# Two graph sum passes: VectorE's one-hots wait for the rows of the unit two ahead in line

## The chip, the cores and the metric

The kernel runs on one core of one Trainium2 chip. The metric is the device time of one launch in microseconds, the median of the runs shown.

## What is computed

The reference is a four-layer graph network on 3,125 nodes of 256 features and 100,000 edges. Each layer adds a graph part, a mixing part and a feed-forward part to x. The change touches the graph parts of layers 1 and 2 alone, which are sums over edges:

```python
# layer 1
index = row * N_EDGE_TYPE + edge_type
sums = segment_sum(x[col], index, num_segments=n * N_EDGE_TYPE)
cnt  = segment_sum(ones, index, num_segments=n * N_EDGE_TYPE)
out1 = (sums / maximum(cnt, 1)[:, None]).reshape(n, -1) @ weights
# layer 2
msgs = (x @ W)[row] * norm[:, None]
out2 = segment_sum(msgs, col, num_segments=N) + bias
```

## The kernel before

The edges are sorted by the node that they are summed into (in layer 1 by `src`, in layer 2 by `dst`) and cut into units of 4 chunks of 128 edges. All edges of a unit belong to one tile of 125 nodes. There are 220 units (`UNITS_S`). In layer 1 the table rows are already multiplied by the weights of each edge type, and the mean's share is the weight of the edge. Both layers then run the same function, `build_sums` (L585): layer 1 with the table `rel_table`, layer 2 with the table `el`.

Inside `build_sums` three engines work on the units in order, each with a program written out by hand:

- GpSimd (L593 to L603) issues four indirect DMAs for a unit, one a chunk, that gather 128 rows of 256 floats each into the row buffer u % 10 (`LANES_S`). From the eleventh unit on it first waits for `batch_summed` of the unit ten before, so that the buffer is free. Each DMA raises the semaphore `rows_in` of its buffer by 16.
- VectorE (L605 to L634) makes a unit's four one-hots with `make_hot` (L611): a 128 x 125 matrix a chunk that holds the edge's weight in the column of its node. There are 14 buffers of them (`HOTS_S`). `add` (L619) takes the finished sum of the unit ten before (`BEHIND`) out of PSUM and adds it to the tile's rows in `acc`; at the first unit of a batch of four it waits for `batch_summed`. After each turn VectorE raises `step` by one. VectorE's loop makes the one-hots of unit n and then adds unit n - 10.
- TensorE (L636 to L643) waits for `step` and for the unit's `rows_in`, multiplies the four one-hots with the four row blocks into one PSUM slot of 16, and raises `batch_summed` after every fourth unit (`BATCH`).

So VectorE may make one-hots ahead of the rows, as far as its own additions let it: it stops at the first addition whose batch isn't summed.

Of the kernel before, what the change touches and what calls it, by code (L numbers as in the profile page):

```python
# [16 lines left out]
G = 4  # L17
# [15 lines left out]
LANES_S = 10  # L33
BATCH = 4
HOTS_S = 14
SLOTS_S = 16
BEHIND = 10
HOTS = 4
REC = 4
REC_LANES = 8  # L40
# [39 lines left out]
@contextmanager  # L80
def phase(nc, tag, *names):

    sems = {n: nc.alloc_semaphore(f"{tag}_{n}") for n in names}
    yield sems
    nc.clear_and_free_semaphores(list(sems.values()))
    nc.all_engine_barrier()


def row_of(ap, k):

    return ap.unsqueeze(1).to_broadcast([ap.shape[0], k, ap.shape[1]])


def col_of(ap, n):

    return ap.unsqueeze(2).to_broadcast([ap.shape[0], ap.shape[1], n])
# [483 lines left out]
def batches_of(u):  # L580

    return u // BATCH + 1


def build_sums(nc, c, tag, table, o, w, acc):  # L585

    assert UNITS_S % BATCH == 0 and HOTS_S >= BEHIND + BATCH and SLOTS_S >= BEHIND + BATCH and BATCH % 2 == 0
    with ExitStack() as ctx:
        rows = [ctx.enter_context(nc.sbuf_tensor(f"{tag}_rows{l}", [P, G, D], F32)) for l in range(LANES_S)]
        hot = [ctx.enter_context(nc.sbuf_tensor(f"{tag}_hot{l}", [P, G, R], F32)) for l in range(HOTS_S)]  # L590
        banks = [ctx.enter_context(nc.psum_tensor(f"{tag}_sum{l}", [R, 2, D], F32)) for l in range(SLOTS_S // 2)]
        slot = lambda u: banks[u % SLOTS_S // 2][:, u % 2, :]
        with phase(nc, tag, "cleared", "batch_summed", "step", *[f"rows_in{l}" for l in range(LANES_S)]) as s, nc.Block() as block:  # L593
            @block.gpsimd
            def _(pool):
                for u in range(UNITS_S):
                    l = u % LANES_S
                    if u >= LANES_S:
                        pool.wait_ge(s["batch_summed"], batches_of(u - LANES_S))
                    for g in range(G):  # L600
                        k = u * G + g
                        nc.gpsimd.indirect_dma_start(rows[l][:, g, :], None, table, bass.IndirectOffsetOnAxis(ap=o["row"][:, k:k + 1], axis=0)  # L602
                                                     ).then_inc(s[f"rows_in{l}"], 16)  # L603

            @block.vector  # L605
            def _(dve):
                v = nc.vector
                v.memset(acc[:], 0.0).then_inc(s["cleared"], 1)

                def make_hot(u):  # L610
                    if u >= HOTS_S:  # L611
                        dve.wait_ge(s["batch_summed"], batches_of(u - HOTS_S))
                    for g in range(G):
                        k = u * G + g
                        last = v.tensor_scalar(hot[u % HOTS_S][:, g, :], c["iota"][:, 0:R], o["node"][:, k:k + 1], w[:, k:k + 1], ALU.is_equal, ALU.mult)
                    return last

                def add(u, steps):
                    at = dve.value_load(o["tile"][0:1, u:u + 1], min_val=0, max_val=TILES - 1)  # L619
                    to = acc[:, bass.ds(at, 1), :].rearrange("p t d -> p (t d)")  # L620
                    if u % BATCH == 0:
                        dve.wait_ge(s["batch_summed"], batches_of(u))
                    dve.wait_ge(s["step"], steps)
                    return v.tensor_tensor(to, to, slot(u), ALU.add)  # L624

                dve.wait_ge(s["cleared"], 1)
                for n in range(UNITS_S + BEHIND):
                    if n < UNITS_S:
                        last = make_hot(n)
                    if n >= BEHIND:  # L630
                        last = add(n - BEHIND, n)
                    last.then_inc(s["step"], 1)

            @block.tensor  # L634
            def _(pe):
                for u in range(UNITS_S):  # L636
                    l = u % LANES_S
                    pe.wait_ge(s["step"], u + 1)
                    pe.wait_ge(s[f"rows_in{l}"], 16 * G * (u // LANES_S + 1))
                    for g in range(G):  # L640
                        last = nc.tensor.matmul(slot(u), hot[u % HOTS_S][:, g, :], rows[l][:, g, :], start=(g == 0), stop=(g == G - 1))  # L641
                    if u % BATCH == BATCH - 1:
                        last.then_inc(s["batch_summed"], 1)  # L643
# [22 lines left out]
def mark_hots(nc, c, o, u, hot):  # L666

    return nc.vector.tensor_tensor(hot[u % HOTS][:], row_of(c["iota"][:, 0:R], G), col_of(o["node"][:, u * G:u * G + G], R), ALU.is_equal)

# [6 lines left out]
def build_attend0(nc, c, o, table, to_dst, attn, acc, pairs):  # L676
# [9 lines left out]
    with ExitStack() as ctx:  # L686
        sb = lambda n, sh, d=F32: ctx.enter_context(nc.sbuf_tensor(f"att0_{n}", sh, d))
        ps = lambda n, sh: ctx.enter_context(nc.psum_tensor(f"att0_{n}", sh, F32))
        rows, hot = [sb(f"rows{l}", [P, G, S]) for l in range(LANES_A)], [sb(f"hot{l}", [P, G, R]) for l in range(HOTS)]
        hot_t, mask = [sb(f"hot_t{l}", [R, G * P]) for l in range(TURNED)], [sb(f"mask{l}", [R, G * P]) for l in range(TURNED)]  # L690
# [8 lines left out]
        with phase(nc, "att0", *names) as s, nc.Block() as block:  # L699
# [11 lines left out]
            def _(dve):  # L711
# [7 lines left out]
                def make_hot(u):  # L719
                    if u >= HOTS:  # L720
                        dve.wait_ge(s["summed"], u - HOTS + 1)
                    mark_hots(nc, c, o, u, hot).then_inc(s["hot_ready"], 1)
# [59 lines left out]
            def _(pe):  # L782
                t = nc.tensor

                def turn(u):
# [3 lines left out]
                    for g in range(G):  # L789
                        last = t.transpose(turn_p[:, g * P:(g + 1) * P], hot[u % HOTS][:, g, :], c["ident"][:])  # L790
                    last.then_inc(s["turned"], 1)
# [27 lines left out]
                def add_up(u):  # L819
# [3 lines left out]
                    for g in range(G):  # L823
                        last = t.matmul(sums[u % 2][:, 0:S], hot[u % HOTS][:, g, :], rows[u % LANES_A][:, g, :], start=(g == 0), stop=(g == G - 1))  # L824
                    last.then_inc(s["summed"], 1)
# [2526 lines left out]
```

## Time and profile before

| what | us |
|---|---|
| median of 3 runs | 9699.5 |
| lowest, highest | 9695.85, 9704.59 |
| span of the profiled execution | 10401.4 |
| layer 1: first gather to last addition | 3754.8 to 5012.9 |
| layer 2: first gather | 5544.5 |
| GpSimd busy with gathers of one sum pass | 833.0 |
| TensorE busy with matmuls of both sum passes | 1227.5 |

The profiled execution is one run on its own; its span is longer than the timed runs. Its own time beside the span isn't among the numbers shown. In the timeline a line is a run of equal instructions: its start, its length, the engine, the line in the program, the operation, what it writes and reads, their count, and in brackets how long the engine was idle before it and what ended that.

### The profile page before, as it was taken

How to read it: one execution, taken by the hardware profiler on the slowest of the kernel's cores; microseconds unless marked ns; L12 is line 12 of the kernel's file. 1: busy time of each engine (PE TensorE's matmuls, PEld its weight loads, DVE VectorE, ACT ScalarE, POOL GpSimd, SP SyncE). 2: the span in 40 equal slices, each digit the busy share in tenths (PEclk: the TensorE clock that was granted, in tenths of full speed). 3: DMA queues.
4: the chain of work that ended last, by engine and by line, in shares of the span. 5: the costliest groups of instructions: out<-in, count | busy, mean ns of one | idle time of the engine just before them, and what ended most of it. 6: DMA issues, size and time to landing. Idle time of an engine off the chain costs nothing. (4 is left out here: it accounts for less than half of the span.)

```text
span 10401.4 us, 95746 instructions
## 1 busy us (share of the span) xinstructions
PE 6311.5 (61%) x28050; PEld 4795.7 (46%) x28050; DVE 4856.6 (47%) x13537; ACT 2031.2 (20%) x5038; POOL 4458.2 (43%) x4412
## 2 busy tenths in 40 slices
PE   0001115999996865454665444453965788887699
PEld 0000004888884433333443333342863676776466
DVE  7561216888884532222242222264113566666633
ACT  0000002444443210000120000012212232232322
POOL 0546772666660036666104666602020566664000
PEclk9998557999997986666676666675987777777799
DMA  0001002333330133333102333301960232222000
GB/s 12 6 1 28 7 4 71 83 83 83 83 83 14 46 108 92 94 92 92 35 11 70 94 92 92 92 18 25 316 221 27 77 81 80 80 81 64 11 13 19
DMA packets 404431, 697.45 MB, mean 67 GB/s; under 512 B 154143, under 2 KB 267784, under 8 KB 403421
## 3 DMA queue, kind: packets, MB, share of 16 engines
q0 software_dynamic: 206848, 480.68, 17.1%
q1 hardware_dynamic: 197076, 210.68, 6.3%
q8 instruction: 236, 3.87, 0.2%
q14 instruction: 271, 2.22, 0.1%
HBM read 631.46 MB, written 59.47 MB: 66 GB/s over the span
## 5 line engine op out<-in xcount | busy, mean ns | idle before, releaser
L658 POOL DMA_INDIRECT att_rows<-el_table,dst_order_row x1520 | 1589.4, 1046 | 1067.4 <-issue 387.0
L641 PE MATMUL sum_sum<-sum_rows,sum_hot 128*125 128x256 f32 x3520 | 1227.5, 487 | 1291.4 <-issue 817.1
L641 PEld LDWEIGHTS sum_sum<-sum_rows,sum_hot 128*125 128x125 f32 x3520 | 824.8, 240 | 1694.4 <-issue 1540.9
L602 POOL DMA_INDIRECT sum_rows<-rel_table,src_order_row x880 | 833.0, 947 | 1042.3 <-ACTq L593 629.2
L602 POOL DMA_INDIRECT sum_rows<-el_table,dst_order_row x880 | 833.0, 947 | 956.7 <-ACTq L593 543.7
L554 POOL DMA_INDIRECT dst_order_record<-records,dst_order_row x784 | 813.7, 1038 | 589.2 <-PEq L458 297.1
L624 DVE TENSOR_TENSOR gnn_acc<-gnn_acc,sum_sum 125x256 f32 x440 | 180.6, 410 | 1888.8 <-DMA ffn1e_w<-in_L_ffn_W_dram 938.7
L1136 PE MATMUL att_sum<-att_rows,att_hot 128*125 128x265 f32 x1280 | 429.3, 492 | 36.4 <-ACT att_part L1203 30.5
L800 PE MATMUL att_found<-gnn_to_dst,att_hot_t 125*128 x1760 | 437.8, 392 | 2.5 <-ACT att_hot_t L849 1.8
L658 POOL DMA_INDIRECT dst_order_record<-el_table,dst_order_row x240 | 266.1, 1109 | 400.4 <-SPq L960 240.5
L824 PE MATMUL att_sum<-att_rows,att_hot 128*125 128x261 f32 x1760 | 427.3, 385 | 2.4 <-ACT att_rows L862 2.4
L862 ACT ACTIVATE att_rows<-att_rows,att_p 128x257 f32<-128x257 f32 x880 | 375.8, 498 | 0.0
L1101 PEld LDWEIGHTS att_found<-layer_a_dst,att_hot_t 125*128 125x128 f32 x1760 | 275.9, 227 | 180.6 <-issue 159.4
L1136 PEld LDWEIGHTS att_sum<-att_rows,att_hot 128*125 128x125 f32 x1280 | 293.4, 241 | 114.7 <-issue 46.9
L1101 PE MATMUL att_found<-layer_a_dst,att_hot_t 125*128 x1760 | 254.4, 268 | 140.1 <-issue 84.2
L800 PEld LDWEIGHTS att_found<-gnn_to_dst,att_hot_t 125*128 125x128 f32 x1760 | 319.7, 192 | 38.0 <-issue 3.1
L824 PEld LDWEIGHTS att_sum<-att_rows,att_hot 128*125 128x125 f32 x1760 | 314.2, 188 | 47.8 <-ACT att_rows L862 2.5
L744 DVE CUSTOM_DVE_ANT_0 att_high<-att_high,att_att 128x256 f32<-128x256 f32 x880 | 320.0, 418 | 0.0
L1162 ACT COPY att_hot_t<-att_turn_p 125x512 f32<-125x512 f32 x220 | 129.1, 587 | 802.7 <-PE att_turn_p L1091 461.7
L809 PE MATMUL att_spread_p<-ident,att_score 128*125 128x128 f32 x1760 | 251.6, 286 | 43.2 <-issue 27.2
L739 DVE TENSOR_TENSOR att_high<-att_rows,att_found 128x1024 f32<-128x1024 f32 x220 | 268.7, 1222 | 6.5 <-issue 6.5
L809 PEld LDWEIGHTS att_spread_p<-ident,att_score 128*125 128x125 f32 x1760 | 210.0, 188 | 130.6 <-issue 85.1
(775 smaller groups left out, 12593.2 us busy)
## 6 DMA issues: line engine op xcount, KB each, us to landing
block_w<-in_L_ffn_W_dram SPq DMA_DIRECT2D x112, 512.0 KB, 6.3
block_w<-in_L_ffn_W_dram SPq DMA_DIRECT2D x56, 1024.0 KB
att_rows<-el_table,dst_order_row POOLq DMA_INDIRECT x1520
rel_table<-open_st SPq DMA_DIRECT2D x25, 784.0 KB
sum_rows<-rel_table,src_order_row POOLq DMA_INDIRECT x880
sum_rows<-el_table,dst_order_row POOLq DMA_INDIRECT x880
dst_order_record<-records,dst_order_row POOLq DMA_INDIRECT x784
pairs<-zeros SPq DMA_DIRECT2D x1, 7168.0 KB
```

The source lines that it names most:

```text
L554: nc.gpsimd.indirect_dma_start(o["record"][:, k, :], None, o["records"], bass.IndirectOffsetOnAxis(ap=o["row"][:, k:k + 1], axis=0)).then_ ...
L602: nc.gpsimd.indirect_dma_start(rows[l][:, g, :], None, table, bass.IndirectOffsetOnAxis(ap=o["row"][:, k:k + 1], axis=0)).then_inc(s[f"row ...
L641: last = nc.tensor.matmul(slot(u), hot[u % HOTS_S][:, g, :], rows[l][:, g, :], start=(g == 0), stop=(g == G - 1))
L658: nc.gpsimd.indirect_dma_start(rows[l][:, g, 0:width], None, table, bass.IndirectOffsetOnAxis(ap=o["row"][:, k:k + 1], axis=0)).then_inc(s ...
L739: v.tensor_tensor(high[:], rows[u % LANES_A][:, :, 0:D], found[:], ALU.max).then_inc(s["picked"], 1)
L744: last = v.tensor_tensor_reduce(high[:, g, :], high[:, g, :], att[:], 0.8, 0.0, ALU.mult, ALU.add, score[u % 2][:, g:g + 1])
L800: last = t.matmul(found[:, g, :], hot_t[u % TURNED][:, g * P:(g + 1) * P], nodes_of_unit(to_dst, tile), start=True, stop=True)
L809: last = t.matmul(spread_p[:, g * P:(g + 1) * P], score[u % 2][:, g:g + 1].to_broadcast([P, R]), c["ident"][:], start=True, stop=True)
L824: last = t.matmul(sums[u % 2][:, 0:S], hot[u % HOTS][:, g, :], rows[u % LANES_A][:, g, :], start=(g == 0), stop=(g == G - 1))
L862: last = a.activation(own_rows[:, g, 0:D + 1], own_rows[:, g, 0:D + 1], ACT.Copy, scale=p[u % 2][:, g:g + 1])
L1101: done = t.matmul(found[u % 2][:, g, 0:H], hot_t[u % 2][:, g * P:(g + 1) * P], nodes_of_unit(to_dst, tile), start=True, stop=True)
L1136: done = t.matmul(sums[u % SUMS_B][:, 0:W + 1], hot[u % HOTS_B][:, g, :], rows[u % LANES_B][:, g, :], start=(g == 0), stop=(g == G - 1))
```

## The change

A constant `AHEAD_S = 2` is added. In `make_hot(u)` VectorE waits, from the third unit on, until all four gathers of unit u - 2 have landed, which is 64 increments of that unit's `rows_in` for each use of its buffer. It stands behind the existing wait for a free one-hot buffer and ahead of the four one-hots.

```diff
+AHEAD_S = 2
...
                 def make_hot(u):
                     if u >= HOTS_S:
                         dve.wait_ge(s["batch_summed"], batches_of(u - HOTS_S))
+                    if u >= AHEAD_S:
+                        at = u - AHEAD_S
+                        dve.wait_ge(s[f"rows_in{at % LANES_S}"], 16 * G * (at // LANES_S + 1))
                     for g in range(G):
```

All engines keep their instructions in the same order. What changes on VectorE are the places where it waits. These are VectorE's instructions at the beginning of layer 1's pass, before the change; the name of a semaphore is that of the first stage that used its number, so that `records_stored` stands for `batch_summed` and `dst_sort_chain` for `step`, and x43 is a run of 43 one-hots:

```order
L608 MEMSET gnn_acc 125x6400
L615 TENSOR_SCALAR sum_hot<-iota,src_order_node,src_order_w 128x125 [waits constants_chain]
L615 TENSOR_SCALAR sum_hot<-iota,src_order_node,src_order_w 128x125 x43
L619 TENSOR_LOAD src_order_tile
L619 ISA x2
L624 ISA [waits dst_sort_chain,records_stored]
L624 TENSOR_TENSOR gnn_acc<-gnn_acc,sum_sum 125x256
```

The one-hots of eleven units stand in one run, up to the first addition. The same place after the change, where `open0_kept`, `open0_flipped` and `open0_xt_ready` are `rows_in` of the first three buffers:

```order
L609 MEMSET gnn_acc 125x6400
L619 TENSOR_SCALAR sum_hot<-iota,src_order_node,src_order_w 128x125 [waits constants_chain]
L619 TENSOR_SCALAR sum_hot<-iota,src_order_node,src_order_w 128x125 x7
L619 TENSOR_SCALAR sum_hot<-iota,src_order_node,src_order_w 128x125 [waits open0_kept]
L619 TENSOR_SCALAR sum_hot<-iota,src_order_node,src_order_w 128x125 x3
L619 TENSOR_SCALAR sum_hot<-iota,src_order_node,src_order_w 128x125 [waits open0_flipped]
L619 TENSOR_SCALAR sum_hot<-iota,src_order_node,src_order_w 128x125 x3
L619 TENSOR_SCALAR sum_hot<-iota,src_order_node,src_order_w 128x125 [waits open0_xt_ready]
L619 TENSOR_SCALAR sum_hot<-iota,src_order_node,src_order_w 128x125 x3
```

The run is cut into one of eight one-hots, for units 0 and 1, and then runs of four, each behind a wait for the rows of the unit two before.

## Rows read from the trace of the kernel before

**Rows 1.** The page's head.

```profile
span 10401.4 us, 95746 instructions
```

**Rows 2.** Groups by line, 3754 to 5015: out<-in xcount | busy, mean ns | idle before.

```profile
L602 POOL DMA_INDIRECT sum_rows<-rel_table,src_order_row x880 | 833.0, 947 | 1042.3 <-ACTq L593 629.2 <-issue 259.8 <-DMA ffn0e_w<-in_L_ffn_eW_dram 153.3
L615 DVE TENSOR_SCALAR sum_hot<-iota,src_order_node,src_order_w 128x125 f32<-128x125 f32 x880 | 253.4, 366 | 0.0
L624 DVE TENSOR_TENSOR gnn_acc<-gnn_acc,sum_sum 125x256 f32 x220 | 90.2, 410 | 944.4 <-DMA ffn0e_w<-in_L_ffn_eW_dram 907.6 <-issue 31.9 <-PE sum_sum L641 2.4
```

**Rows 3.** Waits of GpSimd, 3754 to 5015: us in total, times, longest.

```profile
POOL sum_rows L602 <- issue: 259.8, 853, 0.3
POOL sum_rows L602 <- DMA ffn0e_w<-in_L_ffn_eW_dram: 153.3, 26, 8.9
```

**Rows 4.** Line 602 in both passes: durations in ns min/median/max; one of its waits.

```profile
L602 POOL DMA_INDIRECT sum_rows<-rel_table,src_order_row x880: 940/946/1027, 3754.8 to 4999.8; - x176
L602 POOL DMA_INDIRECT sum_rows<-el_table,dst_order_row x880: 940/946/1042, 5544.5 to 6789.5; - x176
...
  DMA ffn1e_w<-in_L_ffn_W_dram: 153.2, 26
```

**Rows 5.** Timeline of all engines, the beginning of layer 1's pass.

```profile
3754.79 0.95 POOL L602 DMA_INDIRECT sum_rows<-rel_table,src_order_row  x1 [629.22 <-ACTq L593]
...
3760.98 11.33 DVE L615 TENSOR_SCALAR sum_hot<-iota,src_order_node,src_order_w 128x125 f32<-128x125 f32 x44
...
3762.14 3.78 PE L641 MATMUL sum_sum<-sum_rows,sum_hot 128*125 128x256 f32 x8 [12.41 <-DVE sum_hot L615]
3762.30 0.99 POOL L602 DMA_INDIRECT sum_rows<-rel_table,src_order_row  x1 [0.30 <-issue]
3763.59 0.95 POOL L602 DMA_INDIRECT sum_rows<-rel_table,src_order_row  x1 [0.30 <-issue]
...
3766.46 3.75 PE L641 MATMUL sum_sum<-sum_rows,sum_hot 128*125 128x256 f32 x8 [0.55 <-DMA sum_rows<-rel_table,src_order_row]
...
3773.73 0.94 POOL L602 DMA_INDIRECT sum_rows<-rel_table,src_order_row  x1 [0.30 <-issue]
```

**Rows 6.** The same timeline, TensorE a little later.

```profile
3781.54 1.96 PE L641 MATMUL sum_sum<-sum_rows,sum_hot 128*125 128x256 f32 x8 [1.59 <-DMA sum_rows<-rel_table,src_order_row]
...
3786.75 3.24 PE L641 MATMUL sum_sum<-sum_rows,sum_hot 128*125 128x256 f32 x8 [3.25 <-DMA sum_rows<-rel_table,src_order_row]
```

**Rows 7.** Stretches: length, busy us (records) by engine, granted clock, DMA share, GB/s.

```profile
core 0: us, PE busy (x) PEld busy (x) DVE busy (x) ACT busy (x) POOL busy (x), PEclk, DMA share, GB/s
3762.10:3770.20 8.10, 7.51 (x16) 4.95 (x16) 8.10 (x33) 0.00 (x0) 6.08 (x7) 0.50 0.34 97
...
3797.60:3833.00 35.40, 9.49 (x17) 4.25 (x15) 5.83 (x20) 0.00 (x0) 20.64 (x22) 0.50 0.29 85
3856.00:3877.00 21.00, 4.86 (x9) 2.56 (x9) 0.00 (x0) 0.00 (x0) 13.22 (x14) 0.50 0.32 94
```

**Rows 8.** Timelines of VectorE and GpSimd around 3879.

```profile
3878.92 0.42 DVE L624 TENSOR_TENSOR gnn_acc<-gnn_acc,sum_sum 125x256 f32 x1 [33.96 <-DMA ffn0e_w<-in_L_ffn_eW_dram]
...
3880.28 0.41 DVE L624 TENSOR_TENSOR gnn_acc<-gnn_acc,sum_sum 125x256 f32 x1
...
3888.85 1.22 DVE L615 TENSOR_SCALAR sum_hot<-iota,src_order_node,src_order_w 128x125 f32<-128x125 f32 x4
...
3879.05 0.95 POOL L602 DMA_INDIRECT sum_rows<-rel_table,src_order_row  x1 [5.79 <-DMA ffn0e_w<-in_L_ffn_eW_dram]
```

**Rows 9.** Timeline of all engines, the end of layer 1's pass.

```profile
4992.83 2.47 PE L641 MATMUL sum_sum<-sum_rows,sum_hot 128*125 128x256 f32 x5 [2.39 <-DMA sum_rows<-rel_table,src_order_row]
...
4999.84 0.95 POOL L602 DMA_INDIRECT sum_rows<-rel_table,src_order_row  x1 [0.30 <-issue]
...
5011.73 0.42 DVE L624 TENSOR_TENSOR gnn_acc<-gnn_acc,sum_sum 125x256 f32 x1 [0.34 <-DVE gnn_acc L624]
5012.49 0.42 DVE L624 TENSOR_TENSOR gnn_acc<-gnn_acc,sum_sum 125x256 f32 x1 [0.34 <-DVE gnn_acc L624]
```

## The prediction

> **What bounds the kernel now.** I read the page first: the profiled execution spans 10401.4 us [rows 1]. The timed runs have a median of 9699.5 us, 701.9 us less, so the profile tells mechanisms and the sum below is a difference, made on the profiled execution and carried to the median. Then the groups by line over the first sum pass. It starts with the first gather at 3754.79 us and ends with the last addition at 5012.9 us [rows 5, 9]. GpSimd issues 880 gathers (L602) of 947 ns and stands idle 259.8 us "issue" between them, 0.30 us each [rows 2, 3]. A unit of four gathers so takes 4 x (0.947 + 0.30) = 4.99 us, and 220 units take 1,098 us. The other 153 us are 26 waits of GpSimd, which the waits view puts down to an unlikely DMA of another stage; what GpSimd waits for there in the code is `batch_summed` [rows 3]. The second pass has the same two figures, 947 ns and 153.2 us [rows 4]. Next the timeline: TensorE begins a unit when its rows have landed, 5.0 us after the one before, and is done with its 8 records in 1.96 us at the full clock, or 3.78 us at half [rows 5, 6]. VectorE is busy 253.4 + 90.2 us of the pass, 1.56 us a unit, and idle for 944 us [rows 2]. So the chain is GpSimd's issue, and behind it TensorE by way of `batch_summed` 26 times in a pass. VectorE is on neither.
>
> One thing in the trace needs care. TensorE has stretches in which it hardly moves: in 21.0 us from 3856 it does 9 matmul records at a granted clock of 0.50 (the 1.2 GHz level), while 16 records at the same clock fit in 8.1 us earlier [rows 7]. So the low level alone doesn't explain them. GpSimd runs out of freed row buffers in each and waits, most often 5.8 us, as at 3879.05 [rows 8]; that is where the 26 waits come from. VectorE shows no busy time at all from 3856 to 3877 [rows 7].
>
> **The change, part by part.** First, 218 waits are added to each pass, one ahead of a unit's four one-hots (units 0 and 1 have none). No instruction changes its place. Behind the wait on VectorE stand the four one-hots of unit n, then the addition of unit n-10, and then the `step` increment for which TensorE waits. The trace of before has no such wait. A wait at which VectorE really sleeps can be bounded by the tail, where additions follow one another 0.76 us apart with 0.34 us idle between two, a self-wait and a register load [rows 9]. A step of VectorE in a burst takes 1.35 us (3878.92 to 3880.28) [rows 8]; with the wait it is 1.35 to 1.69 us (1.35 + 0.34), and a unit has 4.99 us. Its own cost is hidden by GpSimd's issue: 0 us. Without that cover it would be up to 218 x 0.34 = 74 us a pass.
>
> Second, the lead of the one-hots falls. Now VectorE makes 11 units of them in one go (44 in 11.33 us) [rows 5], and later steps on in bursts of eight from 3878.92 to 3890.07, as often as batches come free [rows 8]. After the change the one-hots of unit u begin when the rows of u-2 land and are announced at most 1.69 us later. The rows of u land 2 x 4.99 = 9.98 us after those of u-2. That leaves 9.98 - 1.69 = 8.3 us of slack in every unit: TensorE still waits for the rows last. When TensorE lags, rows are landed far ahead, so the new wait is met already and the older wait, the one for `batch_summed` in the addition, holds VectorE as now. I put 0 us, and 0 to both sides of it: a step of 1.69 us ends before the next rows in any case.
>
> Third, the additions. The addition of unit n-10 stands behind the one-hots of unit n, so it now waits for the rows of n-2 too. Its only reader within the pass is the reuse of a sum slot 16 units on, which is six units later than that addition; and the tail. At the tail, the last gather ends at 5000.79 [rows 9] and its rows land about 1.9 us behind it (unit 1's last issue ended at 3764.54, TensorE began it at 3766.46 [rows 5]), so at 5002.7; those of unit 217 at 5002.7 - 9.98 = 4992.7, and TensorE does begin a unit at 4992.83 [rows 9]. From there VectorE has its last one-hots, 1.69 us, and six additions of 0.76 us, 4.6 us, before those of the last batch: done at 4999.0, 3.7 us before the last rows land. So again 0; if all six were left over, 2 x 4.6 = 9 us for both passes.
>
> Fourth, VectorE beside GpSimd. Issues in the opening burst of one-hots read up to 0.99 us, against 0.94 us once it is over [rows 5], so an issue beside one-hots can cost up to 0.05 us. A burst of four steps is 5.4 us long and touches about 6 issues of 1.25 us; four single steps touch about 2 each, 8. That is 2 more in four units, 110 in a pass, 5.5 us, and 11 us for both passes at most. Below nothing: if spreading took all disturbance away, 947 would become the shortest issue, 940 ns [rows 4], -7 ns x 880 x 2 = -12 us. I take 0: the mean of now, 947, stands 1 ns from the median, 946 [rows 4], so issues beside one-hots weigh little already.
>
> The Trainium skill speaks against the change here: "SBUF — State Buffer", section "Who interferes with whom", says that VectorE's tensor_scalar can enter a two-port mode that locks GpSimd out of a shared port pair for the whole instruction, descriptors of its DMAs included. By that rule each of the 110 newly touched issues could wait a whole one-hot, 0.366 us, 40 us a pass and 81 us for both. The opening burst, 44 one-hots back to back under nine issues, shows 0.05 us and not 0.37, so the trace doesn't bear out a lock of that size.
>
> The sum: 0 + 0 + 0 + (-12 to +11), so 0 on the profiled execution, and 9,700 us for the timed median.
>
> **Rivals.** (a) *VectorE disturbs GpSimd* (slower). If one-hots spread over the whole pass held every one of the 880 issues at 0.99 us in place of 0.947, a pass would be 38 us longer and the kernel 76 us: 9,776 us. It leaves the bound of no change, 19.4 us or 9.7 us a pass, once a further quarter of the issues (9.7 / 38) is held; my count above gives a further eighth (110 of 880). For it: GpSimd's issue is the bound, so each nanosecond counts. Against: VectorE is busy 1.4 of 4.99 us and can't touch all four issues of a unit. The skill's lock ends at much the same time, 9,781 us, and is in this case's chance. (b) *The bursts cause TensorE's slow stretches* (faster). They come 26 times in 220 units, once in eight or nine, and the bursts are of eight steps; one-hots paced by landings would end the bursts. If the stretches are there in the timed runs too, their 153.3 + 153.2 = 306.5 us would go: 9,393 us. Against: the first stretch, at 3797.6 [rows 7], came 25 us after the opening burst had ended (3760.98 + 11.33) [rows 5]; VectorE is idle in the one from 3856 [rows 7]; and the timed runs are 702 us shorter than the profiled one, so that these stalls may be no part of them. A half effect, at 9,550, is in this case. (c) *The wait never ends last for anybody* (no change): if VectorE were late anyway, the wait would be met when reached. The 44 one-hots in a row speak against it for the opening; the time would be the same 9,700 us, so it shares the forecast's side. (d) Something that I don't see lengthens the slow stretches, which already free buffers too late: one gather more in each of the 52 waits, 1.25 us, is 65 us, 9,765 us.
>
> **How the numbers follow.** Forecast, with (c) in it: 0.80. (a) 0.06, (b) 0.10, (d) 0.04. The bound between change and no change is 0.2%, 19.4 us, about what the measurement tells from nothing. My own terms reach from -12 to +11 us, and the runs of before spread from 9695.85 to 9704.59, so the forecast's range is 9,700 - 20 to 9,700 + 20, within the bound on both sides; the rivals, 0.20 together, are left out of it. Hence faster 0.10, same 0.80, slower 0.10.
>
> **What would show it.** Right: in the timeline VectorE's opening shows 8 one-hots and then fours at a distance of 5 us; the additions stand one by one between them; L602 stays at 947 ns give or take 10, and the groups show no idle time of TensorE put down to one-hots beyond the opening of each pass (12 us now). Each step wrong: L602's mean over 0.96 us (fourth part); TensorE idle for `sum_hot` in mid-pass (second); a last addition more than 5 us later behind the last matmul than now (third). The forecast as a whole falls if the timed median leaves 9,680 to 9,720, above all if GpSimd's 26 waits in a pass become fewer or shorter and the timed runs follow, which would be (b).

## The result, and the profile after

The changed kernel takes 9714.98 us, the median of 20 runs (9709.41 to 9727.47). The kernel before takes 9697.58 us, also the median of 20 (9691.43 to 9708.34). The ratio is 1.0018, with a 95% interval of 1.0011 to 1.0024: 17.4 us more, inside the range of 9,680 to 9,720 us and inside the 0.2% that the prediction calls no change, but near its edge, and the interval reaches a little beyond it. The sum had been 0. There is an effect, small and surely above nothing, and it has to be found.

The execution that the rows ahead of the prediction come from, with its span of 10401.4 us [rows 1], was an unusual one: a second profiled execution of the kernel before, 9695.68 us with a span of 9693.6, is like the timed runs. I call it the second profile of before, and the comparisons below are made with it.

The page of the changed kernel, head:

```profile
span 9708.2 us, 96158 instructions
```

This profiled execution took 9709.96 us. The groups by line in the stretch of layer 1's sum pass, changed kernel (out<-in xcount | busy us, mean ns of one | idle before and what ended it), which answer to [rows 2]:

```profile
L603 POOL DMA_INDIRECT sum_rows<-rel_table,src_order_row x880 | 842.9, 958 | 896.1 <-ACTq L594 628.3 <-issue 265.6 <-PE sum_sum L645 2.1
...
L619 DVE TENSOR_SCALAR sum_hot<-iota,src_order_node,src_order_w 128x125 f32<-128x125 f32 x880 | 244.1, 359 | 782.8 <-DMA sum_rows<-rel_table,src_order_row 782.7
L628 DVE TENSOR_TENSOR gnn_acc<-gnn_acc,sum_sum 125x256 f32 x220 | 90.9, 413 | 10.4 <-PE sum_sum L645 6.3 <-DVE gnn_acc L628 3.0 <-issue 0.4
```

VectorE now waits for rows, 782.7 us of a pass. And the gather, which was issued in 947 ns, takes 958. The same line in the second pass, from the page:

```profile
L603 POOL DMA_INDIRECT sum_rows<-el_table,dst_order_row x880 | 844.5, 960 | 806.6 <-ACTq L594 538.8
```

The waits in the first pass, changed kernel (us in total, times, longest), which answer to [rows 3]:

```profile
DVE sum_hot L619 <- DMA sum_rows<-rel_table,src_order_row: 782.7, 217, 5.0
...
PE sum_sum L645 <- DMA sum_rows<-rel_table,src_order_row: 477.0, 218, 4.5
POOL sum_rows L603 <- issue: 265.6, 872, 0.3
...
PE sum_sum L645 <- DVE sum_hot L619: 12.4, 1, 12.4
...
POOL sum_rows L603 <- PE sum_sum L645: 2.1, 7, 0.3
```

TensorE waits for one-hots once, 12.4 us at the opening of the pass, as before [rows 5]; in mid-pass only rows hold it. GpSimd waits for nothing but its own issue. The 26 long waits of [rows 3] are not there. They are not there in the second profile of before either, as its groups by line show:

```profile
L602 POOL DMA_INDIRECT sum_rows<-rel_table,src_order_row x880 | 836.0, 950 | 899.6 <-ACTq L593 631.9 <-issue 265.0 <-PE sum_sum L641 2.7
L602 POOL DMA_INDIRECT sum_rows<-el_table,dst_order_row x880 | 835.5, 949 | 807.1 <-ACTq L593 539.3 <-issue 265.6 <-PE sum_sum L641 2.1
```

Of the 153 us in each pass nothing is left. So the change has not removed them: they belonged to that one execution. From the first gather to the last addition a pass takes 1110.4 and 1110.0 us in the second profile of before (in the first one 1258), and 1117.4 and 1120.7 us in the changed kernel: 7.0 + 10.7 = 17.7 us, as much as the 17.4 us measured; these two executions themselves differ by 14.6 us in span, so nothing is left for the rest of the kernel. The gathers' busy time has grown by 842.9 - 836.0 = 6.9 and 844.5 - 835.5 = 9.0 us, 15.9 of the 17.7. The rest lies behind the last gather of the second pass, which ends 8.5 us ahead of the last addition, and 6.7 us ahead of it before. So nearly all of the cost is in GpSimd's issue, the bound of the passes.

Where in the issue? The timeline of the changed kernel in mid-pass (start, length, engine, line, operation, count, idle before):

```profile
3611.26 0.95 POOL L603 DMA_INDIRECT sum_rows<-rel_table,src_order_row  x1 [0.30 <-issue]
3611.62 1.11 DVE L619 TENSOR_SCALAR sum_hot<-iota,src_order_node,src_order_w 128x125 f32<-128x125 f32 x4 [3.31 <-DMA sum_rows<-rel_table,src_order_row]
...
3611.66 1.96 PE L645 MATMUL sum_sum<-sum_rows,sum_hot 128*125 128x256 f32 x8 [1.52 <-DMA sum_rows<-rel_table,src_order_row]
3612.51 1.03 POOL L603 DMA_INDIRECT sum_rows<-rel_table,src_order_row  x1 [0.30 <-issue]
3612.65 0.41 DVE L628 TENSOR_TENSOR gnn_acc<-gnn_acc,sum_sum 125x256 f32 x1
3613.85 0.95 POOL L603 DMA_INDIRECT sum_rows<-rel_table,src_order_row  x1 [0.30 <-issue]
3615.10 0.95 POOL L603 DMA_INDIRECT sum_rows<-rel_table,src_order_row  x1 [0.30 <-issue]
3616.35 0.95 POOL L603 DMA_INDIRECT sum_rows<-rel_table,src_order_row  x1 [0.30 <-issue]
3616.67 1.11 DVE L619 TENSOR_SCALAR sum_hot<-iota,src_order_node,src_order_w 128x125 f32<-128x125 f32 x4 [3.62 <-DMA sum_rows<-rel_table,src_order_row]
...
3617.60 0.99 POOL L603 DMA_INDIRECT sum_rows<-rel_table,src_order_row  x1 [0.30 <-issue]
```

Of four issues one is longer, 1.03 and 0.99 us in place of 0.95, and in both units it is the one that starts while the last of the four one-hots runs. The four start 0.257 us apart, so the last one starts 0.77 us behind the first: at 3612.39 in the first unit, 0.12 us ahead of the issue at 3612.51, and at 3617.44 in the second, 0.16 us ahead of that at 3617.60. I took all 1760 issues of the two passes from the same records, and sorted those that start beside a unit's last one-hot by how far behind its start they begin:

| start behind the last one-hot's start, ns | issues | mean length, ns | longer than 960 ns |
|---|---|---|---|
| 80 to 100 | 27 | 1057 | 26 |
| 100 to 120 | 44 | 1043 | 44 |
| 120 to 140 | 78 | 1025 | 78 |
| 140 to 160 | 88 | 1005 | 88 |
| 160 to 180 | 93 | 985 | 93 |
| 180 to 200 | 53 | 967 | 42 |
| 200 to 220 | 19 | 949 | 0 |
| 220 to 260 | 14 | 946 | 0 |

An issue of 946 ns that starts in this window ends as if it had started 0.21 us behind the one-hot. With the middle of each range and the mean's excess over 946, 90 + 111, 130 + 79, 170 + 39, 190 + 21 are all near 210 ns. I call that lengthening the hold. Of the 1760 issues 372 are over 960 ns; in the second profile of before 118 are.

Why should nearly every unit meet it? VectorE's row of one-hots now begins at a landing (at 3611.62 the rows have landed, and TensorE begins the same unit at 3611.66); a landing follows the end of a unit's fourth issue by a steady time, and the issues follow one another in steps of 1.25 us. So the row stands at the same place between two issues in unit after unit. If that place is a bad one, it is bad some 200 times in a pass. Before, VectorE's rows come in bursts when a batch comes free, with four steps 1.35 us apart, and meet the issues at places that differ. This was the theory to test; the rivals were that the shorter lead of the one-hots costs the time, that the addition holds the issue, and that VectorE's work as such does, wherever it stands.

### The profile page after: what moved, and what is told of

Read it like the earlier page. It is cut to its first block and busy times, and to the rows that moved or that the text cites. A ratio compares the mean times of both kernels' runs of the same rounds, so it can differ in the third digit from the quotient of the medians.

```text
span 9708.2 us, 96158 instructions
## 1 busy us (share of the span) xinstructions
PE 6252.1 (64%) x28050; PEld 4787.4 (49%) x28050; DVE 4875.1 (50%) x13537; ACT 2039.2 (21%) x5038; POOL 4520.6 (47%) x4412
## 5 line engine op out<-in xcount | busy, mean ns | idle before, releaser
L645 PE MATMUL sum_sum<-sum_rows,sum_hot 128*125 128x256 f32 x3520 | 1256.6, 520 | 984.4 <-DMA sum_rows<-el_table,dst_order_row 484.0
L645 PEld LDWEIGHTS sum_sum<-sum_rows,sum_hot 128*125 128x125 f32 x3520 | 862.1, 257 | 1378.9 <-issue 1183.5
L603 POOL DMA_INDIRECT sum_rows<-rel_table,src_order_row x880 | 842.9, 958 | 896.1 <-ACTq L594 628.3
L603 POOL DMA_INDIRECT sum_rows<-el_table,dst_order_row x880 | 844.5, 960 | 806.6 <-ACTq L594 538.8
L555 POOL DMA_INDIRECT dst_order_record<-records,dst_order_row x784 | 834.8, 1065 | 582.5 <-PEq L459 297.0
L619 DVE TENSOR_SCALAR sum_hot<-iota,dst_order_node,dst_order_record 128x125 f32<-128x125 f32 x880 | 243.8, 357 | 783.9 <-DMA sum_rows<-el_table,dst_order_row 781.6
L619 DVE TENSOR_SCALAR sum_hot<-iota,src_order_node,src_order_w 128x125 f32<-128x125 f32 x880 | 244.1, 359 | 782.8 <-DMA sum_rows<-rel_table,src_order_row 782.7
L794 PE MATMUL att_turn_p<-ident,att_hot 128*125 128x128 f32 x880 | 155.1, 299 | 380.7 <-DVE att_hot L672 370.0
L794 PEld LDWEIGHTS att_turn_p<-ident,att_hot 128*125 128x125 f32 x880 | 113.5, 188 | 422.5 <-DVE att_hot L672 422.3
```

What stands on the lines that cost most here:

```text
L555: nc.gpsimd.indirect_dma_start(o["record"][:, k, :], None, o["records"], bass.IndirectOffsetOnAxis(ap=o["row"][:, k:k + 1], axis=0)).then_ ...
```

## The experiments

**The kernel before, once more.** No edit.

> The kernel before, unchanged, to have its profile from the same chip. Phase theory: GpSimd's gathers in the sum passes (L602) have a mean of about 947 ns against 958 and 960 ns in the changed kernel, 11 to 13 ns x 880 or 10 to 12 us a pass, which is the whole measured difference of 17.4 us within some 5 us. If the first profile's slow stretches of TensorE were part of that one execution only, they are absent here, GpSimd has no waits of 5.8 us, and the span is near 9698 us; if they belong to the kernel, they are here again and the span is near 10400 us.

Measured: 9695.68 us, a span of 9693.6, no long waits of GpSimd. The gathers read 950 and 949 ns and not 947, so that 8 and 10 ns each are left for the change. The stretch from 3548 to 4640 us of this profile (length, busy us and records of PE, PEld, DVE, ACT, POOL, then granted clock, DMA share, GB/s):

```profile
3548.00:4640.00 1092.00, 626.09 (x1744) 429.88 (x1744) 308.46 (x1097) 0.00 (x0) 826.71 (x871) 0.76 0.36 105
```

TensorE does 1744 records in 1,092 us at a mean granted clock of 0.76, where [rows 7] had 9 in 21 us at 0.50. The slow stretches of the first profile are not in this execution, whose time is that of the timed runs. VectorE still works in bursts; its timeline, second profile of before:

```profile
3608.15 0.42 DVE L624 TENSOR_TENSOR gnn_acc<-gnn_acc,sum_sum 125x256 f32 x1 [15.82 <-PE sum_sum L641]
3608.48 1.14 DVE L615 TENSOR_SCALAR sum_hot<-iota,src_order_node,src_order_w 128x125 f32<-128x125 f32 x4
3609.54 0.41 DVE L624 TENSOR_TENSOR gnn_acc<-gnn_acc,sum_sum 125x256 f32 x1
...
3626.50 0.42 DVE L624 TENSOR_TENSOR gnn_acc<-gnn_acc,sum_sum 125x256 f32 x1 [12.73 <-PE sum_sum L641]
```

One burst of four steps for each batch; ahead of these two VectorE was idle for 15.8 and 12.7 us, until TensorE had summed the next batch.

**The lead of the one-hots.** They wait for the unit six ahead instead of two, so that they are made four units earlier.

```diff
-AHEAD_S = 2
+AHEAD_S = 6
```

> AHEAD_S is 6 in place of 2: one-hots are made four units, some 20 us, earlier, but still when a unit's rows land. Phase theory (the last one-hot of a step stands over the start of a gather issue, because every step starts at the same distance behind a landing, and holds that issue by some 53 ns once a unit): no change against the kernel with 2, mean gather 956 to 961 ns, ratio to the kernel before 1.001 to 1.0025. Lead theory (two units are too little, TensorE gets its one-hots late): the loss goes, ratio 0.9995 to 1.0005.

Measured: 1.0017 [1.0008, 1.0026] against the kernel before, as slow as the change. The gather, from its groups by line:

```profile
L603 POOL DMA_INDIRECT sum_rows<-el_table,dst_order_row x880 | 843.5, 959 | 808.1 <-ACTq L594 540.4 <-issue 265.3 <-PE sum_sum L645 2.4
```

959 ns. A lead of six units helps nothing, so the lead was not what cost the time. Any landing has the same place among the issues, and the hold stays: 348 issues over 960 ns.

**The place of the row, moved.** A load of a tile number into a register that nobody reads, between the new wait and the one-hots, makes VectorE begin later and changes nothing else. I ran two loads first and then, with the reading below, one and three.

```diff
                         dve.wait_ge(s[f"rows_in{at % LANES_S}"], 16 * G * (at // LANES_S + 1))
+                        for _ in range(2):
+                            dve.value_load(o["tile"][0:1, u:u + 1], min_val=0, max_val=TILES - 1)
```

> The changed kernel, with two extra register loads on VectorE between the new wait and the one-hots, which move each step of VectorE about 1.1 us later within the same unit; the number of one-hots and of steps, and the pacing by landings, stay. Phase theory: the gather issue then begins some 250 to 400 ns behind the start of the last one-hot, not 80 to 200, and isn't held; mean gather 945 to 949 ns, ratio to the kernel before 0.9995 to 1.0006. Spread theory (every issue beside one-hots costs, and pacing spreads them over more issues): as the changed kernel or worse, 1.0015 or more. Lead theory: later one-hots are worse, 1.0018 or more.

Measured: 1.0017 [1.0008, 1.0026]. The hold did not go, and the expectation missed. The timeline of this kernel shows why:

```profile
3603.88 3.51 PE L647 MATMUL sum_sum<-sum_rows,sum_hot 128*125 128x256 f32 x8 [2.99 <-DMA sum_rows<-rel_table,src_order_row]
3604.79 0.95 POOL L603 DMA_INDIRECT sum_rows<-rel_table,src_order_row  x1 [0.30 <-issue]
3605.08 1.11 DVE L621 TENSOR_SCALAR sum_hot<-iota,src_order_node,src_order_w 128x125 f32<-128x125 f32 x4 [3.59 <-issue]
3606.04 0.97 POOL L603 DMA_INDIRECT sum_rows<-rel_table,src_order_row  x1 [0.30 <-issue]
```

The rows land by 3603.88, where TensorE begins, and the one-hots start at 3605.08: the two loads take 1.20 us. That is nearly the distance of two issues, 3606.04 - 3604.79 = 1.25 us. The row has moved by one whole step and meets the next issue at the same place: the last one-hot starts at 3605.85, 0.19 us ahead of the issue at 3606.04. If the theory holds, the effect is periodic: one load must remove the hold, and three must too.

The same edit with one load, `range(1)`:

> The changed kernel with one extra register load between the new wait and the one-hots, so that each step of VectorE comes about 0.6 us later, half the distance of 1.25 us between gather issues; two loads had moved it by nearly a whole distance, onto the start of the next issue. Phase theory: no issue starts while the last one-hot runs; mean gather 945 to 949 ns, sum passes of about 1104 us from first gather to the end of the last, 6 to 8 us less each than in the changed kernel, ratio to the kernel before 0.9988 to 1.0003. Spread theory: as the changed kernel, mean gather 957 to 961 ns and ratio 1.0015 or more.

Measured: 1.0001 [0.9992, 1.0010], and so no slower than before. The gathers of the first pass, and the timeline of this kernel in mid-pass:

```profile
L603 POOL DMA_INDIRECT sum_rows<-rel_table,src_order_row x880 | 832.1, 946 | 896.0 <-ACTq L594 628.2 <-issue 265.6 <-PE sum_sum L647 2.1
```

```profile
3604.54 3.54 PE L647 MATMUL sum_sum<-sum_rows,sum_hot 128*125 128x256 f32 x8 [3.02 <-DMA sum_rows<-rel_table,src_order_row]
3605.13 1.11 DVE L621 TENSOR_SCALAR sum_hot<-iota,src_order_node,src_order_w 128x125 f32<-128x125 f32 x4 [3.60 <-DMA sum_rows<-rel_table,src_order_row]
3605.43 0.94 POOL L603 DMA_INDIRECT sum_rows<-rel_table,src_order_row  x1 [0.30 <-issue]
3606.16 0.41 DVE L630 TENSOR_TENSOR gnn_acc<-gnn_acc,sum_sum 125x256 f32 x1
3606.68 0.94 POOL L603 DMA_INDIRECT sum_rows<-rel_table,src_order_row  x1 [0.30 <-issue]
```

The one-hots start 0.59 us behind the landing. The last one starts at 3605.90; the issues begin 0.47 us ahead of that and 0.78 behind, and both take 0.94. VectorE does the same instructions, and 218 loads a pass on top, and costs GpSimd nothing: that VectorE's work disturbs the issue wherever it stands is refuted. 13 issues of 1760 are over 960 ns. From the first gather to the end of the last one the passes take 1099.8 and 1100.2 us, 11 and 12 us less than in the changed kernel. That is more than the 6 to 8 us expected, since the smaller hold of the kernel before (1103.7 and 1103.3 us) is gone too.

The changed kernel again, one load and three loads, all beside the same runs of the kernel before:

> The changed kernel again, beside one and three register loads on the same chip. Phase theory: mean gather 956 to 962 ns, ratio to the kernel before 1.0010 to 1.0026, and slower than the kernels with one and three loads by 10 to 25 us. If the difference from the kernel with one load had come from the chip, it is gone here.

> One register load ahead of the one-hots, again, on the same chip as the changed kernel. Phase theory: mean gather 945 to 950 ns, ratio 0.9990 to 1.0005.

> Three register loads ahead of the one-hots, about 1.8 us. Phase theory: the effect is periodic in the distance of issues, 1.25 us: no load is held, one isn't, two are held, so three aren't; mean gather 945 to 950 ns, ratio 0.9990 to 1.0007. A theory in which a later step is simply better or worse has three as good as or worse than two loads by its own trend: two had 954 to 956 ns, better than none, so a smooth trend gives 950 to 953 ns for three, and 956 for one, where 946 was measured.

Measured: 1.0018 [1.0009, 1.0027] with no load, 1.0002 [0.9993, 1.0011] with one, 0.9994 [0.9985, 1.0003] with three. The gathers of the first pass with no load:

```profile
L603 POOL DMA_INDIRECT sum_rows<-rel_table,src_order_row x880 | 841.1, 956 | 892.4 <-ACTq L594 624.7 <-issue 265.3 <-PE sum_sum L645 2.4
```

The same group with three loads:

```profile
L603 POOL DMA_INDIRECT sum_rows<-rel_table,src_order_row x880 | 833.4, 947 | 892.3 <-ACTq L594 624.5 <-issue 265.0 <-PE sum_sum L647 2.7
```

On the same chip the changed kernel is 13 us slower than the one with one load and 21 us slower than the one with three, so the difference is not the chip's. With no load the issues are held, with one they are not, with two they are, with three they are not. Nor is it the number of issues that run beside a one-hot: in the trace with three loads 727 of 1760 overlap one and 40 are over 960 ns, in the second profile of before 539 and 118. It isn't how late the row is that decides, but its place within a step of 1.25 us.

**The kind of instruction.** The one-hots are made by an instruction that reads a second tile in SBUF (the weight as an operand of the whole row) in place of two scalars for each partition.

```diff
-                        last = v.tensor_scalar(hot[u % HOTS_S][:, g, :], c["iota"][:, 0:R], o["node"][:, k:k + 1], w[:, k:k + 1], ALU.is_equal, ALU.mult)
+                        last = v.scalar_tensor_tensor(hot[u % HOTS_S][:, g, :], c["iota"][:, 0:R], o["node"][:, k:k + 1], w[:, k:k + 1].to_broadcast([P, R]), ALU.is_equal, ALU.mult)
```

> The changed kernel with each one-hot made by a scalar_tensor_tensor whose weight comes as a broadcast tensor, so an instruction with two inputs from SBUF, in place of tensor_scalar with one; result and number are the same. If tensor_scalar's use of a port that GpSimd shares is what holds the issue (the Trainium skill, SBUF - State Buffer, Who interferes with whom, has tensor_scalar among the instructions that can take it), the hold goes or changes its size: mean gather 945 to 949 ns, ratio to the kernel before 0.9995 to 1.0006. If any VectorE instruction at that place holds the issue, or the second input takes the port as well, the mean gather stays at 955 to 962 ns and the ratio at 1.0012 to 1.0025.

Measured: 1.0022 [1.0013, 1.0031]. The timeline of this kernel:

```profile
3606.80 1.13 DVE L619 SCALAR_TENSOR_TENSOR sum_hot<-iota,src_order_node,src_order_w 128x125 f32<-128x125 f32 x4 [3.25 <-DMA sum_rows<-rel_table,src_order_row]
...
3607.75 1.00 POOL L603 DMA_INDIRECT sum_rows<-rel_table,src_order_row  x1 [0.30 <-issue]
```

The hold is as it was, 383 issues over 960 ns. So it is not particular to `tensor_scalar`. The Trainium skill, "SBUF — State Buffer", section "Who interferes with whom", names both forms: a `tensor_scalar` can enter a two-port mode, in which it takes the port pair that VectorE shares with GpSimd for its whole length if it is the first to issue, and an instruction with two inputs in SBUF contends with a GpSimd instruction that reads SBUF. Both runs agree with that in so far as GpSimd's issue is held (372 and 383 of 1760); neither shows that the port is the cause. A form that by that page takes no share of the pair was not tried, so the cause of the hold inside the two engines stays open.

**The addition.** VectorE adds first and makes the one-hots behind that, both behind the new wait. `wait_rows` is the wait of the change as a function; the part of the edit that is left out keeps it in `make_hot` for units 2 to 9, which have no addition.

```diff
...
                 for n in range(UNITS_S + BEHIND):
-                    if n < UNITS_S:
-                        last = make_hot(n)
                     if n >= BEHIND:
+                        if AHEAD_S <= n < UNITS_S:
+                            wait_rows(n)
                         last = add(n - BEHIND, n)
+                    if n < UNITS_S:
+                        last = make_hot(n)
```

> The changed kernel with each step of VectorE turned round: behind the wait for the rows comes the addition of the unit ten before, then the four one-hots, which so come some 0.33 us later. Phase theory: the issue starts while the third one-hot of four runs, with a fourth behind it; the last one-hot is over before the next issue starts; mean gather 945 to 952 ns and ratio 0.9990 to 1.0008. If it is the addition next to the issue's start that holds it and not the last one-hot, the hold goes too; then the few steps without an addition (units 2 to 9 of each pass) of the changed kernel should show no hold, and one of them does. Spread theory: as the changed kernel, 1.0015 or more.

Measured: 0.9993 [0.9984, 1.0002]. The timeline of this kernel:

```profile
3604.48 0.42 DVE L631 TENSOR_TENSOR gnn_acc<-gnn_acc,sum_sum 125x256 f32 x1 [3.63 <-DMA sum_rows<-rel_table,src_order_row]
3604.75 0.95 POOL L603 DMA_INDIRECT sum_rows<-rel_table,src_order_row  x1 [0.30 <-issue]
3604.82 1.10 DVE L622 TENSOR_SCALAR sum_hot<-iota,src_order_node,src_order_w 128x125 f32<-128x125 f32 x4
3606.00 0.95 POOL L603 DMA_INDIRECT sum_rows<-rel_table,src_order_row  x1 [0.30 <-issue]
```

An issue that starts 0.27 us behind the addition's start is not held, nor is the next one, which starts 0.41 us behind the last one-hot's. The mean of 949 ns is here the median too, and 11 issues are over 960. That the addition is not what holds the issue is seen also in the changed kernel itself, where unit 9 has no addition yet and the issue behind its last one-hot, begun 179 ns after that one's start, takes 973 ns. In its second pass the same holds for units 7 and 8, with 1017 and 982 ns.

**The wait once in a batch.** Only every fourth unit waits for rows; the other three follow as additions let them.

```diff
-                    if u >= AHEAD_S:
+                    if u >= AHEAD_S and u % BATCH == 0:
```

> The changed kernel with the new wait at every fourth unit alone, so that VectorE makes four units of one-hots in a burst whose start stands at a landing. Phase theory: of the sixteen issues of four units one or two start under the last one-hot of a step, against four in the changed kernel, since steps of 1.35 us drift against issues of 1.25 us; mean gather 947 to 953 ns, ratio to the kernel before 0.9995 to 1.0010. Spread theory: fewer issues beside one-hots than with single steps, the same direction, mean gather near the 949.9 ns of the kernel before.

Measured: 0.9998 [0.9989, 1.0007], gathers of 951 ns and 95 issues over 960 ns in both passes. With a quarter of the waits the bursts are back, and with them the number of before.

All profiled executions together. The passes are measured from the first gather to the last addition; "held" are issues over 960 ns of the 1760 of both passes, and "excess" the sum of all 1760 over their median (946 ns; 949 in the two that are marked):

| kernel | ratio to before | gather, mean ns, both passes | passes, us | held | excess, us |
|---|---|---|---|---|---|
| before, second profile | 1 | 950, 949 | 1110.4, 1110.0 | 118 | 6.5 |
| the change | 1.0018 [1.0011, 1.0024] | 958, 960 | 1117.4, 1120.7 | 372 | 22.4 |
| the change, again | 1.0018 [1.0009, 1.0027] | 956, 959 | 1117.1, 1120.0 | 352 | 20.1 |
| lead of six | 1.0017 [1.0008, 1.0026] | 957, 959 | 1117.9, 1119.6 | 348 | 20.4 |
| one load later | 1.0001 [0.9992, 1.0010] | 946, 946 | 1108.3, 1108.0 | 13 | -0.4 |
| one load later, again | 1.0002 [0.9993, 1.0011] | 946, 946 | 1106.7, 1108.0 | 11 | -0.3 |
| two loads later | 1.0017 [1.0008, 1.0026] | 954, 955 | 1114.7, 1116.7 | 306 | 15.7 |
| three loads later | 0.9994 [0.9985, 1.0003] | 947, 947 | 1108.4, 1109.0 | 40 | 1.5 |
| two inputs in SBUF | 1.0022 [1.0013, 1.0031] | 960, 962 | 1120.6, 1122.8 | 383 | 26.0 |
| addition first | 0.9993 [0.9984, 1.0002] | 949, 949 (949) | 1111.0, 1109.7 | 11 | -0.5 |
| wait once in a batch | 0.9998 [0.9989, 1.0007] | 951, 951 (949) | 1113.3, 1113.2 | 95 | 3.5 |

The kernels fall into two groups: those with 300 issues held and more are slower by 0.17 to 0.22%, with intervals that leave out 1; those with fewer than 120 have intervals that hold it. The change's excess over before's is 22.4 - 6.5 = 15.9 us, of 17.4 measured. Three loads and the addition first are the fastest, by 6 to 7 us in the middle of their intervals, which is about before's own excess of 6.5; but both intervals reach beyond 1, so no version here is shown to beat the kernel before.

**Which of the two waits.** The starts of VectorE's instructions in the same traces show another side of the hold. Of the issues that start 80 to 200 ns behind the start of any one-hot, 371 of 385 are over 960 ns in the changed kernel, but only 112 of 275 in the second profile of before. Beside 154 of the other 163 VectorE waits instead: its next instruction begins 0.18 us behind the start of the issue, and later than its usual step of 0.255 us. Both cases stand next to each other in the kernel that waits once in a batch:

```profile
3660.12 1.11 DVE L619 TENSOR_SCALAR sum_hot<-iota,src_order_node,src_order_w 128x125 f32<-128x125 f32 x4 [14.47 <-DMA sum_rows<-rel_table,src_order_row]
...
3661.07 0.97 POOL L603 DMA_INDIRECT sum_rows<-rel_table,src_order_row  x1 [0.30 <-issue]
...
3661.47 1.14 DVE L619 TENSOR_SCALAR sum_hot<-iota,src_order_node,src_order_w 128x125 f32<-128x125 f32 x4
3662.35 0.94 POOL L603 DMA_INDIRECT sum_rows<-rel_table,src_order_row  x1 [0.30 <-issue]
3662.53 0.41 DVE L628 TENSOR_TENSOR gnn_acc<-gnn_acc,sum_sum 125x256 f32 x1
```

The last one-hot of the first row starts at 3660.89, and the issue 0.18 us behind it takes 0.97. The last one of the second row starts at 3662.24; the issue 0.11 us behind it takes 0.94, the row is 1.14 us long in place of 1.11, and the addition begins 0.18 us behind the issue. In the first row of a burst, ahead of which VectorE was idle for over half a microsecond, 80 of 84 such issues are held in this kernel and 53 of 64 in the second profile of before; in later rows it is 9 of 210 and 59 of 211. In the changed kernel every row is a first row. So the bursts cost less in part because VectorE waits in most of their later rows, which costs nothing, as VectorE isn't the bound. What decides which of the two waits is not shown, and being a first row is not enough: with one load every row is one, and only 12 of 67 such issues are held.

## Why the prediction was right, and where its working was not

The forecast of no change held, and the time lies in the range. But the sum's own terms ended at +11 us, and 17.4 were measured. What held is the range, which was set at the bound of no change, 20 us to each side. To that extent it was luck.

*First, the cost of the wait itself.* Put at 0, and right. VectorE sleeps 217 times in the first pass, 782.7 us, and TensorE never waits for one-hots in mid-pass. The cover, GpSimd's issue of 5 us a unit, was there.

*Second, the lead.* Right: one wait for one-hots, 12.4 us, at the opening. The run with a lead of six, as slow as the change, shows that the lead isn't what cost the 17 us.

*Third, the additions and the tail.* Right. The end of the first pass in the changed kernel, which answers to [rows 9]:

```profile
4652.56 1.96 PE L645 MATMUL sum_sum<-sum_rows,sum_hot 128*125 128x256 f32 x8 [1.41 <-DMA sum_rows<-rel_table,src_order_row]
4654.67 0.42 DVE L628 TENSOR_TENSOR gnn_acc<-gnn_acc,sum_sum 125x256 f32 x1 [6.31 <-PE sum_sum L645]
...
4656.95 0.42 DVE L628 TENSOR_TENSOR gnn_acc<-gnn_acc,sum_sum 125x256 f32 x1 [0.34 <-DVE gnn_acc L628]
```

Four additions are left behind the last matmul, 0.76 us apart, and none of the six older ones.

*Fourth, VectorE beside GpSimd.* This is the term that was mis-sized. It said that an issue beside one-hots costs up to 0.05 us, that 110 more in a pass would be touched, and took 0 in a range of -12 to +11 us; it measured 15.9 us. Two things failed in it. The count took the touched issues as spread evenly and asked how many there are more. What decides is where beside a one-hot an issue starts, and which of the two then waits. The window is some 0.1 us wide of the 0.257 between two one-hots, and work paced by landings meets the issues at one place, in the window in most units or in few. In it start 385 issues of the changed kernel and 275 of the second profile of before; the larger difference is that 371 of the first and 112 of the second are held. Four single steps were counted to touch 8 issues for 6 of a burst; whether these 8 cost all or nothing could not be had from a count. And the price, 0.05 us, came from the opening burst [rows 5], whose issues begin at another place, the one of 0.99 us 36 ns behind a one-hot's start; in the window it goes up to 1057 - 946 = 0.11 us. The upper bound, had it taken one held issue in each of 218 units, would have been 218 x 0.11 x 2 = 48 us.

The sentence on the mean and the median of [rows 4], 947 and 946, from which I took that issues beside one-hots weigh little, rested on the unusual execution: there VectorE stood idle for long stretches [rows 7], and 212 issues began in the window, of which 58 were held, for 275 and 112 in the second profile. That one has 950 and 949 with the same median, 946.

The rule of the Trainium skill that spoke against the change ("SBUF — State Buffer", section "Who interferes with whom") had the direction right, which the prediction set aside. Its size, by the working of the prediction 81 us, is not what the runs show: a held issue waits not a whole one-hot of 0.36 us but until about 0.21 us behind its start, which is 0.11 us at most, and 17.7 us in all.

*The rivals.* (a) VectorE disturbs GpSimd: its mechanism is what happened, at less than a quarter of its price of 76 us; instead of every issue at 0.99 us, some 370 of 1760 are held, by 0.06 us on average (22.4 us / 372). The bound from which it was to decide, 9.7 us a pass or 19.4 for both, was just not reached: 7.0 + 10.7 = 17.7 us. (b) and (d), the slow stretches of TensorE: refuted by the second profile of before, which has the bursts, but neither stretches nor long waits. The prediction had seen that the timed runs were 702 us shorter than the profiled one and gave (b) 0.10 for that; it was right not to carry the 306 us to the timed runs. (c) The wait ends last nowhere: refuted, it ends VectorE's idle time 217 times in a pass.

*The signs that were named.* VectorE's opening shows twelve one-hots in one go and not eight, since VectorE clears `acc` until 3546.07 and the rows of unit 0 have landed before the first eight are done. Then come the fours, 5 us apart:

```profile
3546.11 3.15 DVE L619 TENSOR_SCALAR sum_hot<-iota,src_order_node,src_order_w 128x125 f32<-128x125 f32 x12
3551.40 1.11 DVE L619 TENSOR_SCALAR sum_hot<-iota,src_order_node,src_order_w 128x125 f32<-128x125 f32 x4 [2.14 <-DMA sum_rows<-rel_table,src_order_row]
3556.41 1.11 DVE L619 TENSOR_SCALAR sum_hot<-iota,src_order_node,src_order_w 128x125 f32<-128x125 f32 x4 [3.90 <-DMA sum_rows<-rel_table,src_order_row]
```

"L602 stays at 947 give or take 10" read 958 and 960, just outside, and "over 0.96 us" was just not met. A bound of 10 ns was too coarse: 9 ns x 1760 issues on the bound are 16 us, the whole effect.

## What to carry to other kernels

Work that is paced by an engine's own landings repeats its place against that engine's instructions. A small hold, which the bursts met in 118 of 1760 issues, was then met in over 300 or in 40 and fewer, by the place alone. Look at single instructions of the bounding engine beside the other engine's starts, sort their lengths by the distance, and try a shift of half a step before the pacing itself is judged. And where the profiled execution is far from the timed runs, take a second profile before a term is sized from it: here the stalls of the first, 306 us, were in no other profile.

## What the runs showed of the hardware

An indirect gather of 128 rows, undisturbed, takes GpSimd 946 ns and 0.30 us to the next. Beside a single row of one-hots of VectorE (128 x 125, f32, 0.36 us each) it was held, but for one or two issues a trace, only where it started some 80 to 200 ns behind a one-hot's start (60 to 220 with two inputs), and then until about 0.21 us behind that start; an issue that starts up to 0.08 us behind a one-hot (305 of them with one load, 945 ns on average) or 0.22 us behind (946) isn't held. In the window one of the two waits, and it can be VectorE, whose next instruction then begins 0.18 us behind the issue's start. The first three one-hots of a row hold issues too: in the second profile of before 84 issues over 960 ns started behind one of these, and 34 behind a last one. The window is not the whole of it: six of these 118, in the unbroken runs of one-hots that open the two passes, start 6 to 21 ns behind a one-hot and take 964 to 972 ns. What the issue does in that tenth of a microsecond, what makes the one or the other wait, and whether a shared port is behind it, no run shows.
